# A graph layer and a routed mixture of experts in one kernel: the pace at which finished groups are dealt among the last tiles, the cuts of the tile list, and the queue of six stores

## The reference

```python
def _L0_gnn_ref(x, adjacency, epsilon, W1, b1, rms_weight, W2, b2):
    neighbor_sum = jnp.einsum('bnm,bmd->bnd', adjacency, x)
    agg = epsilon * x + neighbor_sum
    h = jnp.einsum('bnd,dh->bnh', agg, W1) + b1
    h = jax.nn.silu(_rmsnorm(h, rms_weight))
    return jnp.einsum('bnh,hd->bnd', h, W2) + b2

def _L0_ffn_ref(x, gate_w, gate_b, w1, b1, w2, b2, gamma, beta):
    topk_vals, topk_idx = jax.lax.top_k(x @ gate_w + gate_b, 2)
    topk_w = jax.nn.softmax(topk_vals, axis=-1)
    h = jax.nn.relu(jnp.einsum('bsh,ehf->bsef', x, w1) + b1)
    expert_out = jnp.einsum('bsef,efh->bseh', h, w2) + b2
    sel = jnp.take_along_axis(expert_out, topk_idx[:, :, :, None], axis=2)
    y = x + jnp.sum(topk_w[..., None] * sel, axis=2)
    return layernorm(y) * gamma + beta          # mean and variance over the last axis

x = x + _L0_gnn_ref(_layernorm(x), adj, ...)     # x is (128, 128, 128): batch, node, D
x = x + _L0_ffn_ref(_layernorm(x), ...)          # 16 experts, two per token, D 128, F 256
```

## Time and profile before

| | us |
|---|---|
| median of 3 runs | 956.09 |
| lowest, highest | 949.24, 960.18 |
| the profiled execution | 954.74 |
| its span, first to last instruction | 952.8 |
| outside the span | 1.94 |

### The profile page before, as it was taken

One profiled execution on the slowest core, in us unless ns is written; L12 is line 12 of the kernel. 1 busy time (PEld: TensorE's weight loads), 2 busy tenths in 40 slices (PEclk: granted clock), 3 DMA queues, 4 the chain that ended last, 5 costly groups with the idle time before them and its releaser, 6 DMA issues. The chain is left out here.

```text
span 952.8 us, 15722 instructions
## 1 busy us (share of the span) xinstructions
PE 770.1 (81%) x3649; PEld 510.5 (54%) x3650; DVE 596.9 (63%) x2164; ACT 551.5 (58%) x1123; POOL 503.2 (53%) x539
## 2 busy tenths in 40 slices
PE   5999999999999799868879999999887878781000
PEld 3455555555555455446657777777665665661000
DVE  3678888888888677746736656766654444453323
ACT  2799999999999978862223334544433333332121
POOL 2006666666666646666004554544555555457774
PEclk9999999999999999978979999999988888886555
DMA  5354444444444401144656777777765656643222
GB/s 155 132 197 154 152 151 151 151 151 148 155 153 152 135 29 46 46 116 121 187 150 177 190 188 199 205 209 217 210 174 159 173 160 167 174 139 104 74 82 78
DMA packets 136678, 140.77 MB, mean 148 GB/s; under 512 B 18324, under 2 KB 112292, under 8 KB 136359
## 3 DMA queue, kind: packets, MB, share of 16 engines
q1 hardware_dynamic: 117750, 102.67, 36.1%
q0 software_dynamic: 16384, 34.11, 12.8%
q10 hardware_dynamic: 2480, 3.34, 1.1%
HBM read 74.57 MB, written 65.49 MB: 147 GB/s over the span
## 5 line engine op out<-in xcount | busy, mean ns | idle before, releaser
L510 POOL DMA_INDIRECT dispatched<-rows,slot_i x256 | 246.3, 962 | 198.1 <-issue 151.6
L534 POOL DMA_INDIRECT work<-results,place x184 | 178.6, 970 | 191.9 <-issue 69.9
L841 ACT ACTIVATE hid<-bank,wts 128x256 f32<-128x256 f32 x286 | 120.1, 471 | 272.3 <-PE bank L681 272.3
L681 PE MATMUL bank<-tut,wts 128*128 128x256 f32 x572 | 162.4, 410 | 41.5 <-DVE tut L1237 36.5
L696 PE MATMUL bank<-w_all,hid 128*128 x1144 | 177.7, 302 | 0.0
L1257 DVE SCALAR_TENSOR_TENSOR tout<-bank,gate,tin 128x128 f32<-128x128 f32 x274 | 83.5, 347 | 124.0 <-PE bank L696 116.0
L696 PEld LDWEIGHTS bank<-w_all,hid 128*128 128x128 f32 x1144 | 149.3, 204 | 18.3 <-issue 2.5
L681 PEld LDWEIGHTS bank<-tut,wts 128*128 128x128 f32 x572 | 105.5, 205 | 55.6 <-DVE tut L1237 40.1
L560 PE MATMUL bank<-agg,w_sb 128*128 128x512 f32 x256 | 124.5, 609 | 0.0
L575 PE MATMUL bank<-work,w_sb 128*128 128x512 f32 x256 | 116.8, 599 | 3.8 <-ACT work L826 3.8
L534 POOL DMA_INDIRECT rows<-results,place x72 | 71.5, 992 | 49.6 <-issue 27.3
(11 more groups left out here) (190 smaller groups left out, 1030.6 us busy)
## 6 DMA issues: line engine op xcount, KB each, us to landing
tin<-dispatched SPq DMA_DIRECT2D x143, 132.0 KB, 2.8
wts<-in_w_exp SPq DMA_DIRECT2D x143, 129.0 KB, 2.6
results<-tout SPq DMA_DIRECT2D x26, 704.0 KB, 3.2
results<-tout SPq DMA_DIRECT2D x137, 128.0 KB, 2.0
xs<-in_x SPq DMA_DIRECT2D x32, 256.0 KB, 3.1
adj_sb<-in_adj_t SPq DMA_DIRECT2D x32, 256.0 KB, 3.4
out<-agg SPq DMA_DIRECT2D x32, 256.0 KB, 2.5
dispatched<-rows,slot_i POOLq DMA_INDIRECT x256
```

Of the source, the lines that this page charges most:

```text
L510: nc.gpsimd.indirect_dma_start(dispatched, bass.IndirectOffsetOnAxis(slot_i[:, k, n:n + 1], 0), rows[:, k, n // TOPK, n % TOPK, :], None). ...
L534: nc.gpsimd.indirect_dma_start(moe_of(g)[:, n // TOPK, n % TOPK, :], None, results, bass.IndirectOffsetOnAxis(place[:, g, n:n + 1], 0)).th ...
L681: last = nc.tensor.matmul(hid_ps[n % 2][:, c * TILE:(c + 1) * TILE], wts[:, k, c * P:(c + 1) * P], tut[:, n % 2, :], start=True, stop=True)
L841: last = nc.scalar.activation(hid[:, n % 2, c, :], hid_ps[n % 2][:, c * TILE:(c + 1) * TILE], ACT.Relu, bias=wts[:, k, F + c:F + c + 1], s ...
```

## The change

- `SEGS` becomes (1, 3, 5, 8, 11, 14, 17, 20, 24, 29): the first cut is after one group. There are ten cuts, as before. `tiles_by_then` picks them with five instructions where there were three.
- `PACE` = 5: a turn of `post_step` is dealt out over five tiles, of which the fifth has no quarter. `MIX_FROM` is worked out from `SEGS` and goes from 49 to 53; `MIXED` = (143 - 53) // 5 = 18, so `ALONE` goes from 24 to 19.
- The six stores of `store_first` leave SP's queue. ScalarE issues each behind its relus of tiles 12 to 17, on its own DMA queue, after waiting for the table and for that tile's output.

```diff
--- before.py
+++ after.py
@@ -27,11 +27,12 @@
 EARLY_AT = 22
 EARLY_STEP = EARLY_AT + 3
 FULL_AT = 29
-SEGS = (2, 4, 6, 9, 12, 15, 18, 21, 25, FULL_AT)
+SEGS = (1, 3, 5, 8, 11, 14, 17, 20, 24, FULL_AT)
 NS = len(SEGS) + 2
 LAG = 3
 MIX_FROM = max(FIRST + 4 * min(c for c in SEGS if c > g) + E - 1 + LAG - 4 * g for g in range(FULL_AT))
-MIXED = (NT - MIX_FROM) // GB
+PACE = GB + 1
+MIXED = (NT - MIX_FROM) // PACE
 ALONE = MIXED + 1
 RINGM = 9
 BLANK = 11
@@ -318,7 +319,7 @@
             pipeline(eng, tile_step, EARLY, EARLY + 1 + RING2, (NG - 1) // RING2 - 1, MIX_FROM, RING2)
             for t in range(MIX_FROM, NT + 1 + LAG):
                 tile_step(None, t)
-                turn, quarter = divmod(t - MIX_FROM, GB)
+                turn, quarter = divmod(t - MIX_FROM, PACE)
                 if turn < MIXED:
                     post_step(turn, (quarter,))
             for turn in range(MIXED, NG - 1):
@@ -387,11 +388,11 @@
                     .then_inc(tin_in[k], 16)
                 sp.dma_start(wts[:, k], w_exp[bass.ds(w, P), :]).then_inc(wts_in[k], 16)
 
-            def tile_store(n, row, of_tile, kept):
+            def tile_store(n, row):
                 d = nc.s_assert_within(row, 0, (NT - 1) * TILE,
                                        skip_runtime_bounds_check_because="tiles lie densely there")
-                sp.dma_start(results[bass.ds(d, TILE), :].rearrange("(a p) d -> p a d", p=P), of_tile)\
-                    .then_inc(kept, 16)
+                sp.dma_start(results[bass.ds(d, TILE), :].rearrange("(a p) d -> p a d", p=P), tout[:, n % RING2])\
+                    .then_inc(t_kept[n % RING2], 16)
 
             def tile_step(i, t):
                 n = t + 4
@@ -400,7 +401,7 @@
                     got = places_of(table, count(i, n, 1, RING2), 3 if keeps else 2, 0 if loads else 2)
                     if keeps:
                         sp.wait_ge(t_out, count(i, n - RING2 + 1, 1, RING2))
-                        tile_store(n, got[-1], tout[:, n % RING2], t_kept[n % RING2])
+                        tile_store(n, got[-1])
                     if loads:
                         tile_load(n, got[0], got[1])
 
@@ -426,10 +427,7 @@
                 tile_load(n, *places_of(table, n, 2))
 
             def store_alone(n):
-                tile_store(n, places_of(table, n + RING2, 3, 2)[0], tout[:, n % RING2], t_kept[n % RING2])
-
-            def store_first(n):
-                tile_store(n, places_of(table, n + RING2, 3, 2)[0], tout_first[:, n], first_kept)
+                tile_store(n, places_of(table, n + RING2, 3, 2)[0])
 
             for n in range(EARLY, FIRST):
                 load_alone(n)
@@ -443,10 +441,6 @@
             for n in range(FIRST + 1, EARLY + RING2):
                 load_alone(n)
                 store_alone(n - RING2)
-            for n in range(RING2):
-                store_first(n)
-                if n % 2:
-                    tile_step(None, EARLY + RING2 + n // 2 - 4)
 
             def store(g):
                 if 0 <= g < NG:
@@ -455,10 +449,10 @@
 
             lead = EARLY + RING2
             turns = (MIX_FROM - lead) // RING2
-            pipeline(sp, tile_step, EARLY + RING2 + RING2 // 2 - 4, lead, turns, MIX_FROM, RING2)
+            pipeline(sp, tile_step, EARLY + RING2 - 4, lead, turns, MIX_FROM, RING2)
             for t in range(MIX_FROM, NT + RING2 - 4):
                 tile_step(None, t)
-                turn, quarter = divmod(t - MIX_FROM, GB)
+                turn, quarter = divmod(t - MIX_FROM, PACE)
                 if quarter == 3 and turn < MIXED:
                     store(turn - 3)
             for g in range(MIXED - 3, NG):
@@ -842,6 +836,20 @@
                             hid[:, n % 2, c, :], hid_ps[n % 2][:, c * TILE:(c + 1) * TILE], ACT.Relu,
                             bias=wts[:, k, F + c:F + c + 1], scale=2.0)
                     last.then_inc(t_relu, 1)
+                if i is None and EARLY <= t < EARLY + RING2:
+                    store_first(t - EARLY)
+
+            def store_first(n):
+                act.wait_ge(kept_done, 1)
+                act.wait_ge(t_out, n + 1)
+                _, got = nc.values_load_multi_w_load_instructions(
+                    table[0:1, bass.ds(n + RING2, 1), 2:3].rearrange("p t q -> p (t q)"),
+                    engines=[mybir.EngineType.Activation], min_val=0, max_val=E * CAP,
+                    skip_runtime_bounds_check_because="the table holds rows of the tile list alone")
+                d = nc.s_assert_within(got[0], 0, (NT - 1) * TILE,
+                                       skip_runtime_bounds_check_because="tiles lie densely there")
+                act.dma_start(results[bass.ds(d, TILE), :].rearrange("(a p) d -> p a d", p=P), tout_first[:, n])\
+                    .then_inc(first_kept, 16)
 
             step(None, NG)
             step(None, NG + 1, ahead_of_ut=lambda: tile_step(None, 0))
@@ -1003,7 +1011,7 @@
             def tiles_by_then():
                 dve.wait_ge(past_done, 1)
                 past = q_ps[:, 0:FULL_AT * E].rearrange("p (s e) -> p s e", e=E)
-                for first, step, n, at in ((0, 2, 3, 0), (6, 3, 5, 3), (21, 4, 2, 8)):
+                for first, step, n, at in ((0, 1, 1, 0), (1, 2, 2, 1), (5, 3, 5, 3), (20, 4, 1, 8), (24, 5, 1, 9)):
                     link(nc.vector.tensor_scalar(
                         nt_i[:, 0, at:at + n],
                         past[:, first:first + step * n].rearrange("p (b c) e -> p b c e", c=step)[:, :, step - 1],
```

## The result

The changed kernel takes 946.69 us (median of 15 runs, 942.89 to 949.06), the kernel before 956.09 (15 runs, 949.24 to 960.38). The ratio is 0.9907, 95% interval 0.9889 to 0.9926. The forecast was 945, 1.2% faster than the median; measured is 0.9%.

A forecast was written before the change was run, and what follows sets the result against it. It took GpSimd's fetch chain as the bound. Group 19 released by the 140th output at 798.6, plus 144.4 for the free groups, gives a 943.0 span; with 1.94 outside, 944.9, forecast 945, range 936 to 956.

The forecast's parts named there:

- The bound of the kernel before: From 505.65 on, one chain of GpSimd sets the end: 354.7 us of bursts, then 92.4 from group 24.
- The early stores: Six stores leaving SP's queue let every later tile load issue 5.9 us earlier, at no cost to ScalarE.
- Start of the fetches: Group 0's first fetch on GpSimd, released by output of tile 21, comes at about 497, 8.7 us earlier.
- the one-group cut: First cut after one group leaves group 0 needing 22 outputs as before, so it starts no sooner from this.
- Burst groups: GpSimd's 19 groups fetched beside the tiles take 15.39 us each, from 497 to 789.
- The tiles: SP's issue paces them: 2.54 us each from output 52 to output 139, which comes at 797.4.
- Group 19: First free group on GpSimd, ready at 789 but waiting for the 140th output, starts at 798.6.
- The rest: From the first free group to the span's end, 13 free groups instead of 8 take 144.4 us.
- A: Rival: GpSimd's chain is still the whole bound, 140th output there by 789; 935 us, chance 0.10.
- B: Rival: stores moved to ScalarE give nothing back, as relus slip or transfers hold the loads; 951 us, chance 0.11.
- D: Rival: fetches take over 16.4 us a group, so `add_up` stalls again in the last turns; 955, chance 0.07.
- C: Rival: slower, tiles at 2.8 us beside fetches do not pay for five more groups behind them; 967, chance 0.10.

The follow-up runs named there:

- the unedited change: The whole change exactly as in the diff, against the kernel before: 946.69 us, ratio 0.9907; run again on the third chip, 946.58 us, ratio 0.9873.
- e1_stores: Kernel before with only the six stores of `store_first` moved to ScalarE's queue, old cuts and four tiles a turn: 950.83 us, ratio 0.9946.
- e2_pace: Kernel before with only five tiles a turn instead of four, old cuts and the six stores left on SP: 953.82 us, ratio 0.9967.

## Why the prediction was right

*The bound of the kernel before.* GpSimd's chain from its first fetch on: shown. With the stores alone the 43 us of waits stay and group 24 again starts with no wait; the end moves with the chain.

*The early stores.* The mechanism held: loads come sooner by about what the stores took on SP. The term was a little too large. From the load of tile 12 to that of tile 21 the kernel before takes 29.2 us; the unedited change takes 25.2 in its first profile and 23.9 in its second, the stores alone 24.1. So 5.1 to 5.3 come back, 4.1 in the first profile, against the 5.9 of the sum. In the first profile one issue on SP took longer:

```profile
479.24 0.40 SPq L387 DMA_DIRECT2D tin<-dispatched  x1
479.82 1.91 SPq L389 DMA_DIRECT2D wts<-in_w_exp  x1
482.60 0.40 SPq L394 DMA_DIRECT2D results<-tout  x1
483.18 0.37 SPq L387 DMA_DIRECT2D tin<-dispatched  x1
```

An issue of 1.91 instead of some 0.35, for which the profile names no cause. That they cost ScalarE nothing was right.

*Start of the fetches*: forecast 497, measured 500.11. Of the 3.1 us, 1.8 lie ahead of the change's place: tile 12 is loaded at 463.24 instead of 461.45. The two more instructions of VectorE account for no more than some 0.4 of that (five in 1.08 us where three took 0.70). Leaving the second chip out, that load comes anywhere from 459.6 to 465.6 across the kernels of this study, in no order with their edits.

The prediction's 8.7 us at the start hold a second term that it did not name. Only 5.7 of them are earlier loads. The other 3 come from counting 11.4 us from the load of tile 21 to its output, where the profile before has 14.5 (490.69 to 505.2). In that profile TensorE ran at the lower of its two clock levels for some 10 us. Its busy time there, two transposes that waited for a tile's rows, and the eight matmuls of the second weights before the clock fell and after:

```profile
485.50:496.00 10.50, 8.18 (x32) 6.34 (x33) 2.81 (x9) 1.68 (x4) 0.00 (x0) 0.60 0.58 148
```

```profile
478.58 1.16 PE L696 MATMUL bank<-w_all,hid 128*128 x8
481.43 0.44 PE L670 MATMUL bank<-ident,tin 128*128 128x128 f32 x2 [1.70 <-DMA tin<-dispatched]
...
485.97 0.44 PE L670 MATMUL bank<-ident,tin 128*128 128x128 f32 x2 [1.93 <-DMA tin<-dispatched]
...
493.82 2.08 PE L696 MATMUL bank<-w_all,hid 128*128 x8
```

The two waits fall where SP issues the early stores between its loads, and the clock fell at the second. With the stores alone on ScalarE (`e1_stores`) the same part of the kernel runs at the full clock:

```profile
478.00:497.00 19.00, 18.80 (x112) 13.97 (x111) 12.45 (x40) 6.24 (x15) 0.05 (x1) 1.00 0.66 172
```

So 2.3 of the 5.5 us at the start of the changed kernel are its earlier load of tile 21 (488.40) and 3.2 are the shorter way from there to the first fetch, 11.7 us instead of 15.0. Of the 8.7 us of `e1_stores` they are 5.5 and 3.2. With the stores left on SP (`e2_pace`) the clock was low there for some 3 us only and the same way took 11.8, so the 3.2 us are not lost in every execution. The forecast took them as gained without giving a reason, and they came: that part was luck.

That the one-group cut does not free group 0 held: group 0 starts with the 22nd output in either case, and with the old cuts it started no later.

*Burst groups*: 15.39 forecast, 15.42 measured. Taking 14.78, the mean over a stretch with stalled tiles, would have been wrong.

*The tiles.* Output 139 at 799.9, forecast 797.4, of which 2.9 was there at the start. The pace of 2.54 was 2.52. The size was right and its reason half right, which is luck in part: the prediction took SP's issue as the only bound, and on the third chip 11.4 us of issues less gave 3, since TensorE waited for rows only 2.7 us. The two counts agree because both queues need nearly the same time for a tile. Read as "SP alone", the row on SP's waits misled: a queue that never waits can be one of two bounds.

*Group 19*: forecast 798.6 released by the 140th output, measured 800.74 released by it, after 10.7 us of idle. *The rest*: 144.4 forecast, 143.6 measured. The span is 944.3 against 943.0.

So the stall that was removed was large, 43 us, the tiles ended 56 us sooner, and 9.4 us reached the median. The rest went into five more groups behind the last tile, 52 us, and six tiles a turn (1.9% slower than before) shows that this exchange has an optimum, not a direction. With the pace alone the gain is 0.3%, with the stores alone 0.5%, with both and the old cuts 1.1% on the same chip, and 0.9% and 1.3% for the whole change in its two measurements. Whether the two parts give more together than their sum of 0.9% is not shown: the excess of 0.3% is about as large as the intervals.

The chances fit less well than the time. The prediction gave 0.54 to a gain of over 1% and 0.40 to a change within 1%; the 0.93% of the result lies just within.

Of the rivals: A is out (10.7 us of idle where it wanted 0.30), B is out (relus with the same 1.54), D is out (no wait in `add_up`), and C did not happen here; what the second chip showed fits its mechanism.

## What to carry to other kernels

When work is dealt out beside a loop, two quantities have to meet: when the loop ends, and when the dealt-out engine is ready for what may only follow the loop. The idle ahead of the first thing behind the loop tells which side is late (0.30 on one side of the optimum, 10.7 and 56 on the other), and a looser deal stops paying soon after it appears. Price a removed stall by the chain that ends last, not by its own length, and check a bound read from a queue that never waits by taking work off it.

## What the runs showed of the hardware that was not expected

On one chip the kernel before took 1042.6 instead of 956 to 959. In a variant of the change there, tiles took 2.96 instead of 2.52 with TensorE's clock at 0.98, and a group's fetches were unchanged at 14.8. Two variants that were 1.7% and 1.5% faster than the kernel before on the third chip were 1.8% and 2.9% slower there. Whether that is the chip or the hour was not told apart, and the cause is open. A schedule balanced to 10 us between two engines is balanced for one ratio of their paces.

Eight indirect fetches in flight instead of four took the tiles from 2.96 to 3.98 each on that chip, with fewer bytes a second moved (136 against 179 GB/s) and the DMA engines less busy (51% against 66%). The limit that this meets was not found.

Late loads can cost more than their delay. In the profile before, TensorE waited 1.7 and 1.9 us for the rows of two tiles, its clock fell to the lower level for some 10 us, and eight matmuls took 2.08 us instead of 1.16. With the early stores alone taken off SP neither was seen. It is one profile each, so that the one follows from the other is likely and not shown.
